# The boundary of a two-phase GNN and FFN kernel: first residual rows loaded in the last pair, gathers chained tile by tile, other transfers held

## The reference, cut to what matters

```python
edge_index = stack([src, dst])                       # 5000 edges, 10000 nodes, D = 1024
x = x + gnn(layernorm(x), edge_index, W, b)
x = x + ffn(layernorm(x), base_W, base_b, shared_A, shared_B, routed_A, routed_B, router_W, router_b)
# gnn: h = x @ W.T + b; deg counts row (self edges included); norm = deg[row]**-0.5 * deg[col]**-0.5
#      out = segment_sum(norm * h[col], row)
# ffn: base product with (1024 x 1024), plus low-rank shared and routed parts (rank 16, 6 experts, top 2)
```

## Time and profile before

| what | value |
|---|---|
| median of 3 runs | 2082.25 us (2078.88 to 2083.7) |
| profiled execution | 2083.08 us, span 2081.3 us |
| mean granted clock of TensorE | 0.976 |
| TensorE busy | 1957.5 us (94%) |
| VectorE, ACT, GpSimd busy | 1470.2, 901.6, 922.2 us |
| busy share of DMA, SP's queue and GpSimd's | 31.8%, 7.9% |

### The profile page before, as it was taken

How to read it: one execution, slowest core, us unless ns; L and a number is a source line. 1 busy time by engine, 2 the same in 40 slices (tenths; PEclk the granted TensorE clock), 3 DMA queues, 4 the chain that set the end, 5 groups by cost and what they waited for, 6 DMA issues and landing times.

```text
span 2081.3 us, 31608 instructions
## 1 busy us (share of the span) xinstructions
PE 1957.5 (94%) x9583; PEld 1615.6 (78%) x9583; DVE 1470.2 (71%) x3525; ACT 901.6 (43%) x1533; POOL 922.2 (44%) x954
## 2 busy tenths in 40 slices
PE   7999999999999999934899999999999999999999
PEld 6777777777787777823788888888888888888887
DVE  6877887887876666644677767676767767676775
ACT  4455555555555545522333334333333333333332
POOL 1702444444424500025455555555555555555540
PEclk9999999999999999976999999999999999999999
DMA  6533554554443543482233333333333333333321
GB/s 248 203 115 138 177 185 153 179 183 152 177 142 133 145 152 148 147 269 58 83 91 89 96 98 98 90 100 102 97 85 90 100 84 100 101 99 86 90 68 51
DMA packets 148959, 260.20 MB, mean 125 GB/s; under 512 B 56077, under 2 KB 75357, under 8 KB 148822
## 3 DMA queue, kind: packets, MB, share of 16 engines
q1 hardware_dynamic: 99478, 237.85, 31.8%
q0 software_dynamic: 49344, 20.85, 7.9%
HBM read 273.80 MB, written 129.74 MB: 194 GB/s over the span
## 4 chain that ended last, share of the span: by engine, by line
issue 41%; PE 25%; POOL 23%; DVE 6%; ACT 2%; DMA 2%; POOLq 1%; DVEq 0%; ACTq 0%; SPq 0%
POOL acc L828 10%; PE bo L1489 5%; PE bo L1491 5%; PE bo L1493 5%; POOL piece L797 2%; POOL counted L764 2%; POOL counts L778 2%; POOL xpw L706 2%; POOL slots L785 2%; POOL pw L899 1%; DVE xn L1818 1%; POOL tick_pool L681 1%; PE bt L1539 1%; PE bo L1338 1%; PE bo L1340 1%
## 5 line engine op out<-in xcount | busy, mean ns | idle before, releaser
L828 POOL DMA_INDIRECT acc<-h_rows,row_now x312 | 499.5, 1601 | 113.2 <-issue 113.2
L1349 PE MATMUL bo<-wr_hi,left_hi 128*128 128x512 f32 x1008 | 403.1, 400 | 16.3 <-issue 10.1
L1353 PE MATMUL bo<-wr_hi,left_lo 128*128 128x512 f32 x1008 | 394.7, 392 | 0.0
L1351 PE MATMUL bo<-wr_lo,left_hi 128*128 128x512 f32 x1008 | 394.4, 391 | 0.0
L706 POOL TENSOR_TENSOR xpw<-xpin,neg_half 128x1 f32<-128x1 f32 x79 | 72.7, 920 | 504.2 <-DVE xpin L1660 504.2
L1489 PE MATMUL bo<-wr_hi,sum_hi 128*128 128x512 f32 x624 | 253.1, 406 | 0.0
L1493 PE MATMUL bo<-wr_hi,sum_lo 128*128 128x512 f32 x624 | 247.1, 396 | 0.0
L1491 PE MATMUL bo<-wr_lo,sum_hi 128*128 128x512 f32 x624 | 246.6, 395 | 0.0
L1349 PEld LDWEIGHTS bo<-wr_hi,left_hi 128*128 128x128 f32 x1008 | 190.3, 189 | 66.0 <-issue 29.6
L1353 PEld LDWEIGHTS bo<-wr_hi,left_lo 128*128 128x128 f32 x1008 | 190.1, 189 | 40.6
L1351 PEld LDWEIGHTS bo<-wr_lo,left_hi 128*128 128x128 f32 x1008 | 190.5, 189 | 36.4
(11 more groups left out here) (229 smaller groups left out, 4215.8 us busy)
## 6 DMA issues: line engine op xcount, KB each, us to landing
xn<-x SPq DMA_DIRECT2D x79, 512.0 KB, 4.4
r_rows<-xn SPq DMA_DIRECT2D x79, 512.0 KB, 2.7
acc<-r_rows SPq DMA_DIRECT2D x79, 512.0 KB, 4.3
out<-acc SPq DMA_DIRECT2D x79, 512.0 KB, 3.6
h_rows<-hrow SPq DMA_DIRECT2D x144, 256.0 KB, 2.2
acc<-h_rows,row_now POOLq DMA_INDIRECT x312
wr_raw<-w_t SPq DMA_DIRECT2D x16, 256.0 KB, 6.3
piece<-base_t SPq DMA_DIRECT2D x64, 64.0 KB, 4.2
```

Source lines behind the costliest of these rows:

```text
L828: nc.gpsimd.indirect_dma_start(to[:], None, h_dram, bass.IndirectOffsetOnAxis(ap=at, axis=0), bounds_check=NPAD - 1, oob_is_err=False, com ...
L1349: nc.tensor.matmul(ps, left_hi[n][:, k, :], wr_hi[n][:, k, :], start=False, stop=False, skip_group_check=True)
L1351: nc.tensor.matmul(ps, left_hi[n][:, k, :], wr_lo[n][:, k, :], start=False, stop=False, skip_group_check=True)
L1353: last = nc.tensor.matmul(ps, left_lo[n][:, k, :], wr_hi[n][:, k, :], start=False, stop=(k == 3), skip_group_check=True)
```

## The change

Buffers: acc0 moves to the place of the ranking buffers, acc1 to acc4, acc6 and acc7 into the six xn buffers, acc5 to the place of the bias rows; there are three g buffers, two where acc3 and acc4 will be and one where acc5 will be; bl_raw moves into hrow. So acc0, acc1 and acc2 can be loaded, and the g buffers zeroed, while the last pair runs, since pairs 33 and 34 have left those places.

```diff
+            def first_rest():
+
+                sp.wait_ge(r_stored, 16 * first(PAIRS - 2))
+                sp.dma_start(acc[0][:], r_dram[rows(0), :]).then_inc(r_in[DEEP - 1], 16)
+                load_rest(Pair(0, 0), 0)
...
                     store_part(p - 1, C12)
+                    if p == PAIRS - 1:
+                        first_rest()
                     for t in range(2):
                         store_rest(p - 1, t)
...
                 if p == PAIRS - 1:
+                    sp.wait_ge(un_ok, TILES)
+                    sp.wait_ge(first_set, PAIRS)
+                    sp.wait_ge(third_set, PAIRS)
+                    sp.dma_start(narrow_raw[:], base_t[:, 0:HCOLS].rearrange("(k p) n -> p k n",
+                                                                             p=P)) \
+                        .then_inc(weights_in[7], 16)
                     for n in (T1, T2):
...
                     load_right(B21)
-                    sp.wait_ge(un_ok, TILES)
...
-                    sp.wait_ge(done, product_at(p, T3))
-                    load_right(T2)
                 store_part(p, C21)
             store_part(PAIRS - 1, C12)
+            for v in range(4):
+                sp.wait_ge(part_stored[v], 16 * PAIRS)
+            sp.wait_ge(pair_r_ok, 2 * PAIRS)
+            for a, z in ((0, KLOW - 1), (KLOW - 1, KLOW)):
+                sp.dma_start(bl_raw[a:z, 0:2, :].rearrange("p v n -> p (v n)"),
+                             b_low[a:z, :]).then_inc(bl_in, 16)
+            sp.wait_ge(r_stored, 16 * first(PAIRS - 1))
             for t in range(2):
                 store_rest(PAIRS - 1, t)
...
+            sp.wait_ge(first_added, 3)
+            load_rest(Pair(0, 0), 1)
+            sp.wait_ge(done, product_at(PAIRS - 1, T3))
+            load_right(T2)
+            sp.wait_ge(done, product_at(PAIRS - 1, A22))
+            load_right(T3)
             sp.wait_ge(r_stored, 16 * TILES)
+            load_rest(Pair(0, 0), 2)
+            sp.wait_ge(done, product_at(PAIRS - 1, S4))
             sp.wait_ge(rows_ready, 1)
-            sp.dma_start(acc[0][:], r_dram[rows(0), :]).then_inc(r_in[DEEP - 1], 16)
-            load_rest(Pair(0, 0), 0)
-            for q in range(2):
-                sp.wait_ge(g_first[q], 16)
-            sp.wait_ge(done, product_at(PAIRS - 1, S4))
-            for n in (T3, T4):
-                load_right(n)
-            for a in range(1, 3):
-                load_rest(Pair(0, 0), a)
+            load_right(T4)
...
+            def put_first(q, ok):
+
+                nc.gpsimd.indirect_dma_start(
+                    g[q][:], None, h_dram,
+                    bass.IndirectOffsetOnAxis(ap=row_first[:, q + 1:q + 2], axis=0),
+                    bounds_check=NPAD - 1, oob_is_err=False).then_inc(ok, 16)
...
-            for n in (A12, A22):
-                pool.wait_ge(done, product_at(PAIRS - 1, n))
-            for q in range(2):
-                nc.gpsimd.memset(g[q][:], 0.0).then_inc(g_zeroed, 1)
...
+            pool.wait_ge(first_set, PAIRS)
+            nc.gpsimd.memset(g[2][:], 0.0).then_inc(g_zeroed, 1)
+            pool.wait_ge(r_stored, 16 * first(PAIRS - 1))
+            for q in range(2):
+                nc.gpsimd.memset(g[q][:], 0.0).then_inc(g_zeroed, 1)
...
+            def fill(a, t, r, n):
+
+                before_it = ROUNDS * a + r
+                if before_it > 0:
+                    pool.wait_ge(g_fill[t], 16 * before_it)
+                    carry_wait(n)
+                add_tile(z0, a, t, r, g_fill[t])
+
             carry_wait(14)
-            add_first(0, 0)
-            add_first(1, 2)
-            rest_in(z0, 0)
...
+            add_rows(acc[0], row_first[:, 0:1], g_first[0])
+            for q in range(3):
+                put_first(q, g_first[q])
+            for t in range(2):
+                fill(0, t, 0, 0)
+            fill(0, 0, 1, 32)
             power(0)
+            fill(0, 1, 1, 33)
+            for r in range(2, ROUNDS):
+                for t in range(2):
+                    fill(0, t, r, 30 + 2 * r + t)
             rest_in(z0, 1)
+            fill(1, 0, 0, 38)
+            power(1)
+            fill(1, 1, 0, 39)
+            fill(1, 0, 1, 40)
+            power(2)
+            fill(1, 1, 1, 41)
+            for r in range(2, ROUNDS):
+                for t in range(2):
+                    fill(1, t, r, 38 + 2 * r + t)
             slots_of(z0, 2)
             rest_in(z0, 2)
-            carry_wait(20)
-            add_pair(z0, 1, 2)
+            carry_wait(46)
             add_pair(z0, 2, 0)
-            power(2)
+            power(3)
...
             right_high(B21)
-            for v in range(4):
-                act.wait_ge(part_stored[v], 16 * PAIRS)
-            act.wait_ge(r_stored, 16 * TILES)
             act.wait_ge(weights_in[7], 48)
...
-                dve.wait_ge(r_in[DEEP - 1], 16)
-                for q in range(2):
-                    dve.wait_ge(g_first[q], 32)
+                for q in range(3):
+                    dve.wait_ge(g_first[q], 16 if q else 32)
                     nc.vector.tensor_tensor(acc[0][:], acc[0][:], g[q][:], ALU.add) \
                         .then_inc(first_added, 1)
```

More of the change, by code:

```diff
@@ L323, in gnn_ffn @@
                   for v in range(2)]
-        g = [sb(f"g{q}", [P, D], F32, w_end + 16 * HALF + 8 * HALF * q) for q in range(2)]
         y11, o = place("y11", [P, HALF], F32)
@@ L377, in gnn_ffn @@
         g_in = [sem(f"g_in{q}") for q in range(2)]
-        g_first = [sem(f"g_first{q}") for q in range(2)]
+        g_first = [sem(f"g_first{q}") for q in range(3)]
+        g_fill = [sem(f"g_fill{t}") for t in range(2)]
         piece_in, piece_ok, piece_out = sem("piece_in"), sem("piece_ok"), sem("piece_out")
@@ L575, in store_piece, with load_rest @@
                                  piece[:, n, :]).then_inc(piece_out, 16)
+            def load_rest(s, a):
+                for t in range(2):
+                    sp.dma_start(acc[s.acc(a, t)][:], r_dram[rows(s.tile(a, t)), :]) \
+                        .then_inc(r_in[s.mod(a, DEEP)], 16)
+            def first_rest():
+                sp.wait_ge(r_stored, 16 * first(PAIRS - 2))
+                sp.dma_start(acc[0][:], r_dram[rows(0), :]).then_inc(r_in[DEEP - 1], 16)
+                load_rest(Pair(0, 0), 0)
             store_rows(0)
@@ L894, in _ @@
                     pool.wait_ge(spill_added, 16 * (c + 1))
+                for t in range(3):
+                    pool.dma_start(acc[t][:], r_dram[rows(t), :]).then_inc(spill_added, 16)
+                pool.wait_ge(spill_added, 16 * CHUNKS + 48)
             pool.sem_inc(rows_ready, 1)
@@ L956, in step @@
                 if s.has(3):
-                    added(s, 1, 3)
+                    if s.filled(1):
+                        for t in range(2):
+                            pool.wait_ge(g_fill[t], 32 * ROUNDS)
+                    else:
+                        added(s, 1, 3)
                     slots_of(s, 3)
```

104 lines of the change are left out of this document (42 added, 62 removed).

## The result

| | median | range | runs |
|---|---|---|---|
| changed kernel | 2078.11 us | 2075.43 to 2084.36 | 20 |
| kernel before, beside it | 2083.68 us | 2078.88 to 2087.50 | 20 |
| ratio | 0.9977 | 0.9968 to 0.9986 (95%) | |

The kernel became faster: by 5.6 us by the medians, by 0.23% by the ratio, whose interval leaves out 1. 13.5 to 14 us were forecast, and 2078.11 lies above the range of 2061 to 2077. The profiled execution took 2076.89 us (span 2075.1).

The account below looks back on a forecast made before the run. The prediction took the chain of stores, loads and gathers to tile 1's z between the phases as the bound. z1 13.7 us earlier, perhaps 0.3 lost, gave 13.5 to 14 us off 2082.25: 2068.3 us, range 2061 to 2077.

Parts of the forecast that it names:

- the 5.5 us term: End of first phase: early acc and narrow_raw loads delay T1 in SP's queue, so the phase ends 5.5 us later.
- The rule on DMA queues: Tile 1's gathers: engines alternate queues by packet, so small gathers land in perhaps 4.5 us; sum near 17 us.
- from z1 on the steps shift as a block: Behind tile 1's z: all later steps move earlier together, keeping its 13.7 us, of which 0.3 may be lost.
- C: Follow-up theory, second phase: loop back-edges with their clock drops take the gain.
- B: Follow-up theory, second phase: GpSimd's gather chain nearly fills a step, so any small delay opens a wait.
- just enough; if not, a microsecond or two comes back: GpSimd ahead of tile 4's power: two pairs with ticks and a landing take 11.8 us of 12.6.
- The forecast case: Boundary between phases: shorter chain to tile 1's z gains 10 to 19 us, 2063 to 2072; 55%.
- the last pair pays more: Last pair: T1 8 us late, S4 at half clock, C12 store at 920; gain 5 to 9 us; 16%.
- Hidden: Tile 1's z earlier, but TensorE's longer half clock or late T2 to T4 eat it; within 4 us; 6%.

Follow-up runs that it names:

- e2: Changed kernel with the loads of acc0 to acc2 and narrow_raw issued behind T1 and B22 in the last pair; 2070.44 us, ratio 0.9947 to the kernel before.
- e6: Changed kernel with the loads of acc3 to acc6, T2, T3 and T4 held until three rounds of tile 1 landed; 2078.39 us, ratio 0.9947.
- e3: Kernel before with the second gather pair of tiles 5 and 6 behind the power of tile 3; 2084.39 us, ratio 1.0011.
- e7: Kernel before without the fourth round of gathers from tile 5 on (not the full computation); 2088.76 us, ratio 1.0000.
- e1: Changed kernel with four gathers of tiles 3 and 4 ahead of tile 2's power, tiles 5 and 6's second pair ahead of tile 3's; 2075.95 us, ratio 0.9971.
- e4: Changed kernel as it is, run again for a second trace; 2079.96 us, ratio 0.9984 to the kernel before.
- e8: Changed kernel without the fourth round of gathers from tile 5 on (not the full computation); 2079.18 us, ratio 0.9954 to the kernel before.
- e9: Changed kernel as it is, run again for a third trace; 2077.12 us, ratio 0.9973 to the kernel before.
- e10: Changed kernel with gathers from tile 5 on going tile by tile, each waiting only for its own tile's landing; 2076.75 us, ratio 0.9956.
- e5: Changed kernel with the edits of e1 and e2 together; 2071.91 us, ratio 0.9917 to the kernel before.
- e11: The tile-by-tile gathers of e10 on top of e2; 2068.89 us, ratio 0.9921 to the kernel before.
- e14: Changed kernel with eight pairs in place of four in the second phase's loop body (three back-edges for seven); 2060.20 us, ratio 0.9899.
- e13: Kernel before with eight pairs in place of four in the second phase's loop body (three back-edges for seven); 2076.55 us, ratio 0.9961.

## Why the prediction was wrong

Its boundary was right nearly to the microsecond; its second phase was not.

- **Right.** SP's loads at 887 (said: 888); ACT on T1 at 902.4 (902), 6.0 us late (5 to 6); TensorE's wait for u 8.8 us (8); the first gather at 917.6 (917.4); z of tile 0 at 933.6 (932.9); tile 1's rounds 8.6, 7.2 and then 2.7 us to the landing, whole at 949.5 (948.4, at 5.6 us a landing); z of tile 1 at 953.3 (952), 12.3 us earlier for 13.7; TensorE's wait for z_half 21.8 us (22). Of the 1.4 us that are missing, 0.3 is a slip: the prediction's own terms give 952.25 and 13.4. e2 shows the 5.5 us term by taking it away, e6 that the rounds of tile 1 are dearer than quiet ones by contention with the loads. That it fits to a microsecond is one execution's luck: narrow_t 0 lies at 954.8 to 958.7 in the six traces that have this boundary unedited, and at 967.1 to 970.8 in the four with the boundary of before, 11.7 us apart in the mean.
- **The rule on DMA queues.** From the Trainium skill, "DMA: Bandwidth & Descriptors", the prediction worked out a 17 us gain, with small gathers little dearer in a full queue. Beside the loads the two rounds took 8.6 and 7.2 us, without them 5.0 and 4.6 (e6). The measurement decides against that estimate.
- **Wrong: "from z1 on the steps shift as a block".** This is the step that failed. TensorE's 98% was taken as proof that the second phase is one rigid piece. It has seven waits of 2 us at back-edges (12.5 us in all in the trace of before, unread), and a half-clock stretch of 3.41 us behind each of them or not, which costs 1.7 to 1.9 us; and it has, in some executions, a wait for z_half. The share of drops at the back-edges was higher with the change: 11 of 21 in the traces of before, e3 and e7, and 46 of 49 in the seven traces of the changed kernel's boundary with four pairs in the body (the first trace, e1, e4, e6, e8, e9, e10).
- **Its size.** Three traces have the boundary of before, and three are of the changed kernel as it is. Taken apart by their steps (in us; the two columns in the middle are what the steps take beyond 27.15 each; from the last narrow_t to the end it is 24.0 to 24.1 in all):

| trace | narrow_t 0 | first step | 7 back-edge steps, beyond | drops | 31 other steps, beyond | span |
|---|---|---|---|---|---|---|
| before | 967.1 | 35.7 | 21.2 | 4 | 1.6 | 2081.3 |
| e3 | 967.6 | 36.2 | 17.0 | 1 | 1.6 | 2078.1 |
| e7 | 970.8 | 35.5 | 25.5 | 6 | 1.7 | 2089.2 |
| changed, first | 954.8 | 35.7 | 24.3 | 5 | 4.6 | 2075.1 |
| e4 | 957.9 | 36.6 | 25.3 | 6 | 7.0 | 2082.6 |
| e9 | 955.3 | 36.5 | 26.9 | 7 | 0.9 | 2075.3 |

  In the mean the changed kernel is 12.5 us ahead at narrow_t 0. It loses 0.5 in the first step, 4.2 in the back-edge steps and 2.5 in the others, where the waits for z_half lie with the drops behind them, and 5.2 are left (5.6 by the medians of the first comparison). So in these traces C has the larger part of the loss and B the smaller one. In the first trace alone the back-edges take 3.1 and the step with the wait for z_half 4. Six traces are few: the sum at the back-edges varies by 8.5 us among the first three. The mean clocks that each run lists point the same way. In the runs of e4 and e9 they are 0.9779 and 0.9774, and of before beside them 0.9776 and 0.9772. From 1 minus the clock, times two, times the span, that is 91.8 and 93.8 us at half clock, and 93.2 and 94.9 for before. Between 880 and 1010 us the traces have 71.7 us of it in before and 58.0 in the mean of the changed kernel's three. So some 12.5 us more of half clock lie elsewhere in the changed kernel, and cost about half, 6.3 us, an estimate that holds the drops behind waits for z_half too but not these waits themselves.
- **Half right: GpSimd "just enough; if not, a microsecond or two comes back".** It came back, but not at the powers of tiles 3 and 4, and not in each execution: TensorE waited 2.2 to 3.9 us for z_half in five traces (the first, e1, e4, e5, e6), above all in the step to narrow_t 9, which took 29.6 to 31.6 us there, and in e2 and e9 not at all. In the first trace the pair of gathers that starts at 1183.55 has landed only at 1191.9; GpSimd waits 4.6 us for it, and its next gather starts 12.4 us behind narrow_t 8, where in the trace of before that is 6.5. Whether the waits have a part in the median, e10 can't tell; the table gives them 2.5 us.
- **The rivals.** The forecast case held at the boundary (10 to 19 us, at its lower part). No rival named the loop. By its gain of 5 to 9 us "the last pair pays more" came near, but it was wrong as a mechanism: the last pair paid what the forecast said. "Hidden" named TensorE at half clock for longer, which is right in kind, but it put that at the boundary and left at most 4 us.

**Left open.** Why the changed kernel's back-edges bring the drop nearly always, the first one in all seven traces, where in the three of before it never did. The wait ahead of it is alike (1.7 us in the trace of before, 2.0 in the changed kernel's first). Three traces against seven are few, since the drops within one trace go together (1 in e3, 6 in e7), and e2, e5 and e11, with the shortest boundary, have it 14 times in 21. No run moved the second phase in time alone, so that the change causes the higher share is not shown. And e14 has no drop at all where e13 has two: one trace each, so part of the 16.4 us may be chance. What lets GpSimd's gathers fall behind in one execution and not in the next is open too.

## What to carry to other kernels

A phase that is 98% busy can still hold a term that answers to the change: lay one repeating event of both traces side by side and look for steps that are longer than the rest, before calling it a block. Where a hardware loop's body is long and one engine bounds it, count the back-edges: here each cost 2 us (3 with a longer body), or nearly 4 with the clock drop, and going from seven to one saved more than the whole change at the boundary. Loads that are moved ahead can be put behind the one transfer that someone waits for (e2); here that took back at most 0.5 us of the 5.2.

## What the runs showed of the hardware

- A back-edge of this loop held VectorE for 2.4 and 1.8 us of "issue" (the first one of the changed kernel's first trace) and TensorE for about 2 us, seven times in every trace with four pairs in the body (12.5 to 14.5 us in all), in both kernels. With sixteen pairs in the body the straight code ran without such waits, but for one of 1.7 and one of 1.1 us at the back-edge.
- A wait of 2 us of TensorE is followed, in some executions and not in others, by 3.41 us at 1.2 GHz. With drops at every back-edge they lie 112.6 us apart, four steps; executions of one kernel spread by up to 17 us, and the spans of the kernel before follow their mean clock (correlation -0.87 over 29 runs, -0.92 over 23, -0.82 over 17 and -0.74 over 11, in the four groups).
- Two rounds of gathers for tile 1 beside 5 MB of loads took 8.6 and 7.2 us from start to start, without them 5.0 and 4.6 (e6): some 3 us more each.
